# Cross-attention and feed-forward on one core: probabilities turned by VectorE blocks and transfers between partitions, with half-height fp32 scores

## What is computed

```python
b, s, _ = hidden_q.shape                      # 2, 256; hidden_q = layernorm(x)
q_hk = (hidden_q @ Wq.T).reshape(b, s, H, K)  # H = 16 heads, K = 128
q_big = jnp.einsum('bshk,hkq->bshq', q_hk, w_kc_q)
kv_rope = kv_c * cos[None] + _rotate_half(kv_c) * sin[None]      # 512 rows of 64
q_r = jnp.einsum('bshq,hqr->bhsr', q_big, W_qr)
k_r = jnp.einsum('bld,hdr->bhlr', kv_rope, W_kr)
scores = jnp.einsum('bhsr,bhlr->bhsl', q_r, k_r)
attn = jax.nn.softmax(scores, axis=-1)
ctx_c = jnp.einsum('bhsl,bld->bhsd', attn, kv_rope)
ctx_lat = jnp.einsum('bhsd,hkd->bshk', ctx_c, w_kc_kv)
out = ctx_lat.reshape(b, s, H * K) @ Wo.T
...
x = x + out
x = x + layernorm(x) @ weight.T + bias        # 256 x 256, made from 4-bit planes
```

## Time and profile before

| | before |
|---|---|
| median of 3 runs | 171.62 us (170.46 to 171.63) |
| time of the profiled execution | 170.74 us |
| its span, first to last instruction | 168.6 us |
| PE busy | 157.4 us, 93% |
| DVE busy | 113.1 us, 67% |
| ACT busy | 102.2 us, 61% |
| POOL busy | 57.8 us, 34% |
| mean granted TensorE clock | 0.979 |

### The profile page before, as it was taken

How to read it: one execution, slowest core, us unless ns; L and a number is a source line. 1 busy time by engine, 2 the same in 40 slices (tenths; PEclk the granted TensorE clock), 3 DMA queues, 4 the chain that set the end, 5 groups by cost and what they waited for, 6 DMA issues and landing times.

```text
span 168.6 us, 3810 instructions
## 1 busy us (share of the span) xinstructions
PE 157.4 (93%) x1029; PEld 116.9 (69%) x1029; DVE 113.1 (67%) x290; ACT 102.2 (61%) x245; POOL 57.8 (34%) x89
## 2 busy tenths in 40 slices
PE   7486989999999999999999999999999999999863
PEld 7383658577866776686668576857776868877652
DVE  1485886685588478666758685778556939954782
ACT  3123468684868577946876685868486885633310
POOL 6317135242433334423433342423243221530460
PEclk9957999999999999999999999999999999999999
DMA  4953333533243123322332232131850000000002
GB/s 96 295 91 63 86 59 51 115 66 59 76 66 62 28 77 63 54 71 43 60 60 70 42 63 50 62 55 24 291 208 0 0 4 0 0 0 0 4 31 93
DMA packets 42695, 11.13 MB, mean 66 GB/s; under 512 B 39040, under 2 KB 41984, under 8 KB 42688
## 3 DMA queue, kind: packets, MB, share of 16 engines
q1 hardware_dynamic: 41632, 9.95, 26.8%
q0 software_dynamic: 256, 0.75, 1.4%
q10 hardware_dynamic: 800, 0.33, 0.9%
HBM read 10.50 MB, written 0.52 MB: 65 GB/s over the span
## 4 chain that ended last, share of the span: by engine, by line
PE 62%; DVE 16%; issue 8%; ACT 6%; DMA 3%; POOL 2%; SPq 0%; POOLq 0%; DVEq 0%; ACTq 0%
PE ctxb L773 16%; PE trans L762 10%; PE work L744 9%; PE score L754 7%; PE score L755 6%; PE work L736 5%; ACT probs L415 4%; DVE q_hl L545 3%; PE work L725 3%; DVE w_ffn L591 3%; DMA wk_wkr<-in_L_xattn_w_kc_q_dram 3%; DVE neg_max L551 2%; ACT q_hl L410 2%; PE work L843 2%; PE work L731 2%
## 5 line engine op out<-in xcount | busy, mean ns | idle before, releaser
L357 POOL TENSOR_SCALAR probs<-probs,row_inv 128x512 f32<-128x512 f32 x64 | 45.1, 705 | 90.2 <-DVE row_inv L556 90.2
L415 ACT ACTIVATE probs<-score,neg_max 128x512 f32<-128x512 f32 x64 | 44.0, 688 | 34.3 <-DVE neg_max L551 33.7
L551 DVE TENSOR_REDUCE neg_max<-score 128x1 f32<-128x512 f32 x64 | 43.9, 686 | 13.2 <-PE score L755 11.0
L421 ACT ACTIVATE probs_t<-trans 128x512 f32<-128x512 f32 x64 | 36.9, 590 | 3.7 <-PE trans L762 3.7
L762 PE MATMUL trans<-ident,probs 128*128 128x128 f32 x256 | 39.0, 275 | 0.0
L762 PEld LDWEIGHTS trans<-ident,probs 128*128 128x128 f32 x256 | 30.5, 142 | 9.5 <-issue 3.7
L754 PE MATMUL score<-k_hi,q_hl 128*128 128x512 f32 x62 | 31.1, 502 | 0.3 <-ACT probs L415 0.2
L773 PE MATMUL ctxb<-probs_t,kv 128*64 128x256 f32 x240 | 29.2, 385 | 0.0
L755 PE MATMUL score<-k_lo,q_hl 128*128 128x512 f32 x62 | 24.5, 394 | 0.0
L773 PEld LDWEIGHTS ctxb<-probs_t,kv 128*64 128x64 f32 x240 | 15.9, 136 | 9.1 <-issue 1.5
L545 DVE TENSOR_TENSOR q_hl<-work,q_hl 64x256 fp32r<-64x256 f32 x32 | 13.5, 423 | 8.8 <-ACT q_hl L410 8.4
(11 more groups left out here) (104 smaller groups left out, 137.8 us busy)
## 6 DMA issues: line engine op xcount, KB each, us to landing
wq<-in_L_xattn_Wq_dram SPq DMA_DIRECT2D x8, 256.0 KB, 2.7
...
wk_wkr<-in_L_xattn_w_kc_q_dram SPq DMA_DIRECT2D x23, 64.0 KB, 2.4
...
wqr<-in_L_xattn_W_qr_dram SPq DMA_DIRECT2D x7, 96.0 KB, 2.0
wkv<-in_L_xattn_w_kc_kv_dram SPq DMA_DIRECT2D x8, 64.0 KB, 2.0
...
```

What stands on the lines that cost most here:

```text
L357: pool.tensor_scalar(e, e, row_inv[:, j:j + 1], 1.0, ALU.mult, ALU.mult).then_inc(norm_made, 1)
L415: act.activation(probs[:, j, :], score_bank[j % 2][:], ACT.Exp, bias=neg_max[:, j:j + 1], accum_out=row_sum[:, j:j + 1]).then_inc(exp_made, 1)
L421: act.activation(probs_t[:, b, :, h, tt * P:tt * P + P], trans_bank[j % 2][:].rearrange("p (l t) -> p l t", l=LT), ACT.Copy).then_inc(prob ...
L551: dve.tensor_reduce(neg_max[:, j:j + 1], score_bank[j % 2][:], axis=AX, op=ALU.max, negate=True).then_inc(max_made, 1)
```

## The change

Four things change together.

**Scores.** Queries (`q_t`) and keys (`k_t`) are plain fp32, 64 partitions for each head of the pair, the two heads below each other. `scores(i, s)` makes the two heads' tiles of 128 queries (a **slot**; four slots make a pair) with four matmuls of 256 columns and 64 input partitions, alternately head 0 in the upper and head 1 in the lower half. There are four score banks, two for each slot. The splitting into high and low parts on ACT and DVE is gone.

**Probabilities.** In pairs 0 to 6, PE no longer transposes them. DVE turns the 32 x 32 blocks of each tile into `turned` (`turn_probs`), and when the eight tiles of a pair are done, SP moves the blocks between the partitions into `spread`, with 16 transfers of 32 partitions x 4 KB (2 MB in all). The contexts of pair i-2 are then made in pair i from `spread`. The last pair keeps the transposes on PE.

**Sums and copies.** Two banks hold the sums of the output over all pairs, so `project` runs within the pairs, four products in each. One `work` bank is left for all folding steps. All copies out of PSUM except one are on ACT, also that of the contexts.

**Loads and order.** `wo` is loaded whole in 32 transfers during the first pairs, `wkv` and `W_kr` also at the start. POOL scales the two tiles of a slot after one reciprocal, and its extra semaphore instruction is gone. All loops are written out.

```diff
-SLOT_OF = {N_: 0, Q1: 1, CT_: 2, E_: 3, M_: 4, Q0: 6}
...
-        score_bank = [bank("score0"), bank("score1")]
-        trans_bank = [bank("trans0"), bank("trans1")]
+        score_bank = [bank(f"score{k}") for k in range(4)]
         ctx_bank = bank("ctxb")
-        work = [bank("work0"), bank("work1"), bank("work2")]
-        input_bank = [score_bank[0], ctx_bank]
-        ffn_bank = score_bank + work[:2]
+        work = bank("work")
+        out_bank = [bank("proj0"), bank("proj1")]
+        input_bank = [score_bank[2], out_bank[0]]
+        key_bank = [score_bank[3], out_bank[1]]
+        hidden_bank = [work, ctx_bank]
+        late_bank = [work, work, work, work, score_bank[0], score_bank[1], work, score_bank[2]]
...
+            def load_wo(i):
+                for j in range(K // BK):
+                    sp.dma_start(wo[j * BK:j * BK + BK, :, i * BK:i * BK + BK], wo_dram[i, j, :, :, :])\
+                      .then_inc(ld_wo, 16)
+            def load_keys_side(p):
 
                 sp.wait_ge(wk_turned, p)
...
+            def spread_probs(i):
+                sp.wait_ge(probs_turned, TILES * (i + 1))
+                if i >= 2:
+                    sp.wait_ge(ctx_made, B * (i - 1))
+                for g in range(G):
+                    for k in range(G):
+                        sp.dma_start(
+                            spread[i % 2][k * BK:k * BK + BK, g, :, :, :].rearrange("c j l r -> c (j l r)"),
+                            turned[i % 2][g * BK:g * BK + BK, k, :, :, :].rearrange("c j l r -> c (j l r)"))\
+                          .then_inc(probs_spread[i % 2], 16)
...
+            load_keys_side(1)
+            for h in range(2):
+                for a in range(R // BK):
+                    for d in range(DC // BK):
+                        rows = 64 * h + BK * a
+                        sp.dma_start(wkr[rows:rows + BK, :, d * BK:d * BK + BK], wkr_dram[h, a, d, :, 1:NP, :])\
+                          .then_inc(ld_wkr, 16)
+            load_query_weight(1)
+            sp.dma_start(wkv[:], wkv_dram).then_inc(ld_wkv, 16)
+            for i in range(D // BK):
+                load_wo(i)
+                if i == 3:
+                    load_keys_side(2)
+            load_query_weight(2)
+            for i in range(1, LASTP):
+                spread_probs(i - 1)
+                if i + 2 < NP:
+                    load_keys_side(i + 2)
+                    load_query_weight(i + 2)
...
+            spread_probs(LASTP - 1)
...
-            def normalise(t, j):
-                pool.wait_ge(inv_made, t + 1)
-                pool.sem_inc(inv_seen, 1)
-                e = probs[:, j, :]
-                pool.tensor_scalar(e, e, row_inv[:, j:j + 1], 1.0, ALU.mult, ALU.mult).then_inc(norm_made, 1)
-            with pool.Fori(0, NP) as i:
-                for j in range(TILES):
-                    normalise(TILES * i + j, j)
+            def normalise(u):
+                pool.wait_ge(inv_made, u + 1)
+                for h in range(2):
+                    j = 2 * (u % SLOTS) + h
+                    p = probs[:, j, :]
+                    pool.tensor_scalar(p, p, row_inv[:, j:j + 1], 1.0, ALU.mult, ALU.mult).then_inc(norm_made, 1)
+            for u in range(SLOTS * NP):
+                normalise(u)
...
+            for i in range(LASTP):
+                t = TILES * i
+                if i >= 2:
+                    take_folded_values(i - 2)
+                if i == 0:
+                    take_hq(1)
+                exponentials(t)
+                exponentials(t + 1)
+                take_queries(i, 1)
+                if i == 0:
+                    act.wait_ge(k_transposed, 2)
+                    act.activation(k_t[:, 1, :], key_bank[1][:], ACT.Copy).then_inc(k_taken[1], 1)
+                if i >= 2:
+                    take_contexts(i - 2, 0)
+                take_keys_weight(i + 1)
+                exponentials(t + 2)
+                exponentials(t + 3)
+                if i >= 2:
+                    take_contexts(i - 2, 1)
+                take_folded_keys(i + 1)
+                exponentials(t + 4)
+                exponentials(t + 5)
+                take_folded_queries(i + 1)
+                take_queries(i + 1, 0)
+                exponentials(t + 6)
+                exponentials(t + 7)
...
+            def inverses(u):
+                j = 2 * (u % SLOTS)
+                dve.wait_ge(exp_made, 2 * u + 2)
+                dve.reciprocal(row_inv[:, j:j + 2], row_sum[:, j:j + 2]).then_inc(inv_made, 1)
+            def turn_probs(u):
+                i = u // SLOTS
+                if i >= 2 and u % SLOTS == 0:
+                    dve.wait_ge(probs_spread[i % 2], landed(i - 2))
+                for h in range(2):
+                    j = 2 * (u % SLOTS) + h
+                    dve.wait_ge(norm_made, 2 * u + h + 1)
+                    dve.transpose(turned[i % 2][:, :, j, :, :].rearrange("p k l r -> p l k r"),
+                                  probs[:, j, :]).then_inc(probs_turned, 1)
...
+            for i in range(LASTP):
+                u = SLOTS * i
+                maxima(u)
+                if i >= 1:
+                    inverses(u - 1)
+                    turn_probs(u - 1)
+                turn_wk(i + 1)
+                if i == 0:
+                    turn_wkr()
+                maxima(u + 1)
+                inverses(u)
+                turn_probs(u)
+                maxima(u + 2)
+                inverses(u + 1)
+                turn_probs(u + 1)
+                if i >= 1:
+                    turn_wo(i - 1)
+                maxima(u + 3)
+                inverses(u + 2)
+                turn_probs(u + 2)
...
-            def scores(i, t, j):
-                b, h, tt = tile_of(j)
-                if j % (2 * TT) == 0:
-                    pe.wait_ge(work_taken, q_count(i, b))
-                pe.wait_ge(exp_made, t - 1)
-                q = q_hl[:, 2 * b + h, tt * P:tt * P + P]
-                pe.matmul(score_bank[j % 2][:], q, k_hi[:, b, :], start=True, stop=False)
-                pe.matmul(score_bank[j % 2][:], q, k_lo[:, b, :], start=False, stop=True).then_inc(scored, 1)
-            def transpose_probs(t, j, fresh=False):
-                pe.wait_ge(norm_made, t + 1)
-                if not fresh:
-                    pe.wait_ge(probs_taken, t - 1)
-                for lt in range(LT):
-                    last = pe.transpose(trans_bank[j % 2][:, lt * P:lt * P + P],
-                                        probs[:, j, lt * P:lt * P + P], ident[:])
-                last.then_inc(transposed, 1)
...
+            def scores(i, s):
+                u = SLOTS * i + s
+                b, tt = s // TT, s % TT
+                if tt == 0:
+                    pe.wait_ge(work_taken, work_count(Q1 if b else Q0, i))
+                    if i == 0:
+                        pe.wait_ge(k_taken[b], 1)
+                if u >= 2:
+                    pe.wait_ge(exp_made, 2 * u - 2)
+                for half in range(2):
+                    for h in range(2):
+                        rows = slice(64 * h, 64 * h + 64)
+                        product = pe.matmul(score_bank[2 * (u % 2) + h][:, half * S:half * S + S],
+                                            q_t[rows, b, tt * P:tt * P + P], k_t[rows, b, half * S:half * S + S],
+                                            start=True, stop=True)
+                        if half == 1:
+                            product.then_inc(scored, 1)
...
-                        last = pe.matmul(ctx_bank[64 * h:64 * h + 64, 0:S],
-                                         kv[:, b * LT + lt, h * DC:h * DC + DC], probs_t[:, b, lt, h, :],
-                                         start=(lt == 0), stop=(lt == LT - 1))
+                        if i < LASTP:
+                            columns = spread[i % 2][:, :, 2 * TT * b + h:2 * TT * b + 2 * TT:2, lt, :]\
+                                .rearrange("p g t r -> p t g r")
+                        else:
+                            columns = probs_t[:, b, lt, h, :]
+                        last = pe.matmul(ctx_bank[64 * h:64 * h + 64, 0:S], kv[:, b * LT + lt, h * DC:h * DC + DC],
+                                         columns, start=(lt == 0), stop=(lt == LT - 1))
                 last.then_inc(ctx_made, 1)
...
+            def project(i, b):
+                pe.wait_ge(ctx_taken, B * i + b + 1)
+                for tt in range(TT):
+                    t = TT * b + tt
+                    last = pe.matmul(out_bank[b][:, tt * D:tt * D + D], ctx_t[:, t * P:t * P + P], n_all[:, i, :],
+                                     start=(i == 0 and tt == 0), stop=(i == LASTP), skip_group_check=True)
+                if i == LASTP:
+                    last.then_inc(attn_out, 1)
...
+            for i in range(LASTP):
+                scores(i, 0)
+                if i == 0:
+                    transpose_input(1)
+                queries(i, 1)
+                if i == 0:
+                    transpose_keys(1)
```

(19 more changed lines are left out.)

709 lines of the change are left out of this document (312 added, 397 removed).

## The result

| | before | after |
|---|---|---|
| median | 171.62 us | 184.48 us (183.71 to 186.05) |
| ratio, 95% interval | | 1.078 (1.071 to 1.085) |
| span of the profiled execution | 168.6 us | 182.4 us |
| PE, DVE, ACT busy | 157.4, 113.1, 102.2 us | 143.9, 116.1, 79.5 us |

What follows compares the result with a forecast made beforehand. PE bound the old kernel at 16.00 us a pair; DVE would bind at 15.5. Head -0.8, pair 0 -1.1, six pairs -3.0, `wo` +0.5, tail +1.0, together -3.4, gave 168.2 in the median's terms; forecast 168.0, range 165.0 to 180.

Steps and rivals of the forecast that it cites:

- rival 2: SP's loop of transfers between partitions becomes the bound: pairs 2 to 6 take 17.6 us, time 180; chance 0.14.
- PE's work: PE in a loop pair: 14.2 us, or 14.8 with tiling-mode changes, under DVE's bound.
- Rival 1: Half-height score products do not overlap: 1.72 us a slot, PE 17.3 a pair, time 180; chance 0.10.
- DVE's bound: DVE sets the loop pair: slots of 3.54 us plus weight transposes, taken as 15.5, ends 15.2 and 15.9.
- Rival 4: DVE's scattered block-transpose write is slow, 1.26 us: 2.5 to 5 more a pair, time 185 and more; chance 0.05.
- Transfers: SP's 16 issues a pair take 7.7 us and land 2.4 after issue; hidden, with 2 us of slack.
- Term `wo`: `wo`'s 32 issues on SP's queue from 14 us delay the first 16 transfers: +0.5 us, ends 0 and 3.
- Last pair and tail: After the loop, contexts of pair 6 wait for transfers and ACT's tanh: +1.0 us, ends -2 and +3.
- Rival 3: PE's clock falls in pairs 0 and 1: +2 to +4 us, time 171; chance 0.08.

Runs made afterwards that it cites:

- e13: e5 with DVE's order kept and the three `wk` transfers of pair i+2 issued by ACT, not SP: 169.04 us, 0.987 of before.
- e12: e7_turn_behind with the three `wk` transfers of pair i+2 issued by ACT, one at a time, not SP: 167.33 us, 0.975 of before.
- e1: Changed kernel with `pw`, `nw` and the small inputs issued one or a few at a time behind weights of pairs 4 to 7: 178.02 us, 1.033 of before.
- e4: Changed kernel with the edits of e1 and e3 together: 172.98 us, 1.011 of before.
- e5: e4 with `pw` and `nw` as four 512 KB transfers, one behind the weights of each of pairs 3 to 6: 171.24 us, level with the kernel before.
- e7_turn_behind: e5 with DVE's block transposes of a slot one slot later in its order: 172.76 us, 1.010 of before.
- e3: Changed kernel with `wo` loaded by 4 transfers of 512 KB in place of 32 of 64 KB: 179.31 us, 1.050 of before.
- e6: e5 with nine idle products of 128 columns on PE in each of pairs 0 and 1: 172.57 us, 1.006 of before.

## Why the prediction was wrong

The forecast was faster, and the likeliest time 168.0; rival 2 had 0.14 and gave 180, and the range ended there.

- **PE's work: right.** 14.28 us a pair for 14.2. Rival 1 is refuted: a slot of scores takes 1.06, between the 0.95 taken and the 1.3 from which it decides. Eight records two at a time would be 0.86 (8 x 0.215 / 2), so 0.20 is the most that a change of tiling mode can have cost a slot, where the prediction had 0.16. The Trainium skill ("TensorEngine Tiling (Array Packing)", Key Properties) says that such a change drains TensorE; no run here tells a drain from the rest of the 0.20, and it is off the path in the changed kernel.
- **DVE's bound: right**, shown from both sides: it stays in e13 when SP is relieved, and it falls to 14.1 to 14.7, near PE's work, in the undisturbed pairs of e12. That the mean came out at 15.5 is in part luck: three of the pairs take 15.2 or 15.3, the lower end, and those whose contexts wait 0.90 and 1.43 us for their set take 15.6 and 16.1. The slot is 3.44 (31.39 less 27.95), 0.1 under the 3.54 of the sum. Rival 4 is refuted: 0.71 us a block transpose.
- **Transfers: the step that failed.** The sum had 16 issues at 0.48, taken from eight transfers of `wo`, and found 2 us of slack. The issues take 0.63 to 0.72 in the mean, 10.1 to 11.5 us a set, and 12.2 behind `pw` and `nw`. The row of three `wk` in 2.17, 0.72 each, was the nearer one and bounded it from above; I used the lower end without keeping the other. In steady pairs the slack covered nearly all of this (the waits of 0.42 to 1.43 us). It did not where SP's queue held something else. The 217 GB/s that the prediction quotes for 32 partitions are neither shown nor refuted: 2.1 MB in 10.1 us of issues are 208 GB/s, and half the bytes took as long to issue.
- **Term `wo`, +0.5 with ends 0 and 3: it measured 5.4** (pair 1 at 20.9 for 15.5). The 23 us of issues were in the text, and the landing of the first set at 50 too. Overlooked was `wq` of pair 2, which the program puts behind all 32: the sum followed the set and not each of the transfers moved.
- **Last pair and tail, +1.0 with ends -2 and +3: it measured +12.4.** The nine loads for the feed-forward part stood on SP's queue before as well, when nothing urgent came behind them. Now a set of 16 does. It starts 2.6 us late, takes 12.2 to issue where 10.1 is the least, and lands 4.7 after its last issue where 2.4 to 2.7 is usual; PE waits 7.6 us, and contexts and scores behind it lose 2.3 more to the lower clock (3.68 for 1.93, 1.71 for 1.13). With the loads elsewhere the term is 42.1 to 43.1 (e1, e4, e5, e13), +1.9 to +2.9 and inside its range.
- **Rival 2** had the right resource and the wrong form: not in every pair, but on SP's queue in two places, by issue time in the first and by issue time and bytes in the second. In e7_turn_behind its loop set the pace as written, a set every 17.0 to 17.4 us.
- **Rival 3** (the clock in pairs 0 and 1) came true in pair 1 and was hidden behind the first stall: the clock fell before the wait for `wq`, and it falls there in e3 to e6 and in e12 and e13 too. Its price, +2 to +4 in the prediction, is 2.1 us in pair 1 in the one comparison there is, e5_quarters and e13; in pair 0 none shows.

The failed terms are 4.9 too much in pair 1 and 11.4 in the last, together 16.3 of the 17.2 us between the forecast's 165.2 and the span of 182.4.
